# A recommender tower on one core: three PSUM banks for lookups and one for transposes, three lookups ahead of each pair, and the last pair's transposes set between MLP steps

## The reference, cut to what matters

```python
e = jnp.stack([tbl_f[ids[:, f]] for f in range(26)], axis=1)      # [2048, 26, 128]
sd = einsum('bfd,bd->bf', e, dense)                               # 26 dot products with the dense row
ss = einsum('bfd,bgd->bfg', e, e); pairs = ss[:, iu, ju]          # 325 dot products between rows
h = concat([dense, sd, pairs, dense], axis=1)                     # 607 columns
h = relu(h @ W_top1 + b_top1)                                     # 512
h = relu(h @ W_top2 + b_top2)                                     # 256
y = h @ W_top3                                                    # 1
```

## Time and profile before

| what | value |
|---|---|
| median of 3 runs | 382.65 us (378.37 to 382.66) |
| the profiled execution's own time | 384.98 us |
| its span, first to last instruction | 383.2 us |
| mean granted clock of TensorE | 0.969 |
| busy: PE, PEld | 335.0 us (87%), 283.2 us (74%) |
| busy: POOL, ACT, DVE | 259.3, 201.8, 187.4 us |
| moved by DMA | 40.56 MB, mean 106 GB/s |

### The profile page before, as it was taken

How to read it: one execution, slowest core, us unless ns; L and a number is a source line. 1 busy time by engine, 2 the same in 40 slices (tenths; PEclk the granted TensorE clock), 3 DMA queues, 4 the chain that set the end, 5 groups by cost and what they waited for, 6 DMA issues and landing times.

```text
span 383.2 us, 8100 instructions
## 1 busy us (share of the span) xinstructions
PE 335.0 (87%) x3328; PEld 283.2 (74%) x3328; DVE 187.4 (49%) x444; ACT 201.8 (53%) x260; POOL 259.3 (68%) x262
## 2 busy tenths in 40 slices
PE   0798997859899989979989797979989798988976
PEld 0676777748777768868878586968888687978865
DVE  0798973700487744033587572230578473314011
ACT  3387866714563756635461665735472655655201
POOL 5777777777777777777777777777777777730000
PEclk9999998999999999989999899999999899998989
DMA  7997355442255134622136215542226412340310
GB/s 155 254 255 191 118 191 152 116 132 53 54 122 157 49 76 131 159 83 58 50 92 171 74 48 148 117 129 56 50 60 148 126 49 65 90 122 2 90 38 1
DMA packets 46547, 40.56 MB, mean 106 GB/s; under 512 B 29815, under 2 KB 40559, under 8 KB 46512
## 3 DMA queue, kind: packets, MB, share of 16 engines
q1 hardware_dynamic: 38320, 23.26, 23.4%
q0 software_dynamic: 8192, 16.79, 17.1%
HBM read 34.28 MB, written 5.76 MB: 104 GB/s over the span
## 4 chain that ended last, share of the span: by engine, by line
PE 58%; DMA 16%; SPq 9%; POOL 5%; issue 5%; ACT 4%; DVE 2%; ACTq 0%; DVEq 0%
PE oh_ps L504 23%; PE dot_ps L522 15%; PE mlp_ps L543 11%; DMA dots_scratch<-dots 6%; POOL rows L327 5%; SPq L253 5%; PE mlp_ps L552 5%; PE tr_ps L488 4%; SPq L262 3%; DMA ids_bc<-ids_t_dram 3%; DMA zt<-dots_scratch 3%; ACT feat L352 2%; DMA rows<-tbl_dram,idx_sb 2%; ACT feat L360 1%; DMA dots_scratch<-rows 1%
## 5 line engine op out<-in xcount | busy, mean ns | idle before, releaser
L327 POOL DMA_INDIRECT rows<-tbl_dram,idx_sb x256 | 258.8, 1011 | 79.4 <-issue 75.6
L425 DVE TENSOR_SCALAR onehot<-ids_bc 125x512 fp32r<-125x512 int16 x320 | 125.3, 445 | 32.1 <-PE oh_ps L504 24.0
L504 PE MATMUL oh_ps<-onehot,table_hi 125*128 125x512 f32 x320 | 105.5, 411 | 20.2 <-DVE onehot L425 14.4
L504 PE MATMUL oh_ps<-onehot,table_lo 125*128 125x512 f32 x320 | 101.6, 399 | 0.0
L352 ACT ACTIVATE feat<-tr_ps 128x512 f32<-128x512 f32 x64 | 77.3, 1221 | 31.5 <-PE tr_ps L488 30.8
L504 PEld LDWEIGHTS oh_ps<-onehot,table_hi 125*128 125x128 f32 x320 | 59.3, 195 | 33.7 <-issue 12.9
L360 ACT ACTIVATE feat<-oh_ps 128x512 f32<-128x512 f32 x40 | 48.9, 1222 | 45.9 <-PE oh_ps L504 44.8
L504 PEld LDWEIGHTS oh_ps<-onehot,table_lo 125*128 125x128 f32 x320 | 62.1, 194 | 14.0
L522 PE MATMUL dot_ps<-feat 128*54 128x52 f32 x2048 | 61.0, 220 | 10.4 <-issue 5.0
L522 PEld LDWEIGHTS dot_ps<-feat 128*54 128x54 f32 x2048 | 57.8, 136 | 15.1 <-issue 7.6
L543 PE MATMUL mlp_ps<-zt,w_sb 117*128 117x256 f32 x224 | 54.1, 396 | 8.6 <-DMA zt<-dots_scratch 8.6
(11 more groups left out here) (24 smaller groups left out, 55.6 us busy)
## 6 DMA issues: line engine op xcount, KB each, us to landing
ids_bc<-ids_t_dram SPq DMA_DIRECT2D x40, 128.0 KB
dots_scratch<-dots SPq DMA_DIRECT2D x28, 175.5 KB
rows<-tbl_dram,idx_sb POOLq DMA_INDIRECT x256, 2.7
dots<-tbl_dram SPq DMA_DIRECT2D x5, 480.0 KB
zt<-dots_scratch SPq DMA_DIRECT2D x14, 117.0 KB
w_sb<-tbl_dram SPq DMA_DIRECT2D x3, 480.0 KB
dense_sb<-dense_f_dram SPq DMA_DIRECT2D x8, 128.0 KB
zt<-dense_t_dram SPq DMA_DIRECT2D x7, 128.0 KB
```

The costliest lines, as they stand in the source:

```text
L327: nc.gpsimd.indirect_dma_start(rows[:, g, t, :], None, tables[UNIT[u][k]], bass.IndirectOffsetOnAxis(ap=idx_sb[:, n % 2, g * TILES + t:g * ...
L425: last = nc.vector.tensor_scalar(onehot_part(m, part)[:, c, :], ids_bc[0:TP, m % IDSLOTS, :], float(part * PROWS + c), None, ALU.is_equal)
L504: last = nc.tensor.matmul(oh_ps[:, m % 2, :], table[0:TP, u, row * D:(row + 1) * D], onehot_part(m, part)[:, c, :], start=(table is table_ ...
```

## The change

PSUM is divided anew: `oh_ps` gets three banks and `tr_ps` one. Accordingly a lookup waits for the eviction of the lookup three before it, and `transposes` waits for the eviction of the unit just before it. In the orders, the third lookup `l2` moves from behind the dot products of the previous pair's odd chunk to in front of them, for pairs 1 to 3; its eviction `c2` comes behind `c1`, and DVE makes the parts of three lookups ahead of copying those dot products. In the second half of the last pair, the transposes `b2`, `b3` and `b4` each move one MLP step forward.

```diff
+BANKS = 3
-SECOND = "l0 l1 q4 o0 q5 o1 o2 q6 o3 o4 q7 d0 d1 d2 d3 a0 d4 d5 d6 c0 d7 c1 a1 "
-THEN = "l0 a0 l1 a1 d0 d1 d2 d3 d4 d5 d6 c0 d7 c1 "
-LOOK = ("a2 l2 c2 l3 c3 i6 a3 l4 c4 i7 a4 l5 c5 i8 l6 c6 i9 a5 l7 c7 a6 l8 c8 a7 f l9 c9 "
+SECOND = "l0 l1 l2 q4 o0 q5 o1 o2 q6 o3 o4 q7 d0 d1 d2 d3 a0 d4 d5 d6 c0 d7 c1 c2 a1 "
+THEN = "l0 a0 l1 a1 l2 d0 d1 d2 d3 d4 d5 d6 c0 d7 c1 c2 "
+LOOK = ("a2 l3 c3 i6 a3 l4 c4 i7 a4 l5 c5 i8 l6 c6 i9 a5 l7 c7 a6 l8 c8 a7 f l9 c9 "
         "e0 e1 e2 e3 b0 e4 e5 e6 e7 ")
-REST_LAST = "b1 m0 m1 b2 g m2 m3 b3 m4 b4 b5 b6 b7 "
+REST_LAST = "b1 m0 b2 m1 g m2 b3 m3 b4 m4 b5 b6 b7 "
...
-        tr_ps = ps("tr_ps", [P, 2, 2, CH], fp32)
-        oh_ps = ps("oh_ps", [P, 2, BOTH], fp32)
+        tr_ps = ps("tr_ps", [P, 2, CH], fp32)
+        oh_ps = ps("oh_ps", [P, BANKS, BOTH], fp32)
...
-                    for i in range(PLACES, 2 * PARTS):
+                    for i in range(PLACES, BANKS * PARTS):
                         make_part(NO * j + i // PARTS, i % PARTS)
                     if j == 1:
                         layer3(0)
                     dots_to_sbuf(n - 1)
-                    for i in range(2 * PARTS, NO * PARTS):
+                    for i in range(BANKS * PARTS, NO * PARTS):
...
-                if i >= 2:
-                    pe.wait_ge(transposed_out, i - 1)
+                if i:
+                    pe.wait_ge(transposed_out, i)
...
-                if m >= 2:
-                    pe.wait_ge(looked_up_out, m - 1)
+                if m >= BANKS:
+                    pe.wait_ge(looked_up_out, m + 1 - BANKS)
```

More of the change, by code:

```diff
@@ L351, in transposed_to_feat @@
                 act.wait_ge(transposed, i + 1)
-                nc.scalar.activation(feat_view(n % 2, UNIT[u]), tr_ps[:, i % 2], ACT.Copy
+                nc.scalar.activation(feat_view(n % 2, UNIT[u]), tr_ps[:], ACT.Copy
                                      ).then_inc(transposed_out, 1)
@@ L359, in looked_up_to_feat @@
                 both = feat[:, :, :, ONEHOT[m % NO] + 1]
-                nc.scalar.activation(both, oh_ps[:, m % 2, :].rearrange("p (c b) -> p c b", c=2), ACT.Copy
+                nc.scalar.activation(both, oh_ps[:, m % BANKS, :].rearrange("p (c b) -> p c b", c=2), ACT.Copy
                                      ).then_inc(looked_up_out, 1)
@@ L483, in transposes @@
                     pe.wait_ge(ident_made, 1)
-                if i >= 2:
-                    pe.wait_ge(transposed_out, i - 1)
+                if i:
+                    pe.wait_ge(transposed_out, i)
                 for k in range(2):
                     for t in range(TILES):
-                        last = nc.tensor.transpose(tr_ps[:, i % 2, k, t * P:(t + 1) * P], rows[:, 2 * u + k, t, :],
+                        last = nc.tensor.transpose(tr_ps[:, k, t * P:(t + 1) * P], rows[:, 2 * u + k, t, :],
                                                    ident[:])
@@ L503, in lookup @@
                             row = part * PROWS + c
-                            last = nc.tensor.matmul(oh_ps[:, m % 2, :], table[0:TP, u, row * D:(row + 1) * D],
+                            last = nc.tensor.matmul(oh_ps[:, m % BANKS, :], table[0:TP, u, row * D:(row + 1) * D],
                                                     onehot_part(m, part)[:, c, :],
```

## The result

The changed kernel takes 399.63 us (median of 5 runs, 399.26 to 402.21) against 382.65 before: a ratio of 1.0485 with a 95% interval of 1.044 to 1.0531. The profiled execution took 402.21 us, 17.2 more than the one of before; its span is 399.5 us, 16.3 more.

What follows compares the result with a forecast made beforehand. The prediction took PE's work (335.0 us, 87% of the span) plus its waits as the bound. Its terms, 13.6 - 0.2 + 4.7 + 1.3 + 0.3, gave +19.7 us: 404.7 profiled, 402.4 median, range 395 to 409.

Steps and rivals of the forecast that it cites:

- Term 1: Pairs 2 and 3: a4 waits for a3's eviction behind late ids, and l2 delays c0; +6.8 us a pair, +13.6.
- Term 2: End of pair 0: b2 and b3 wait for evictions, but three lookups cover the wait for z; -0.2 us.
- Term 3: Pair 1: a2 waits for a1's eviction, a4 for a3's, and a lookup behind runs slowed; +4.7 us.
- Term 4: Last rows: evictions of b5, b6 and b7 come in series before the last dot products; +1.3 us.
- pair 0: Possible eviction stalls where the margin is thin because ACT also splits tables; +0.3 us taken.
- B: Rival: one bank for transposes costs nothing, so no change; +0.7 us, 383.4 us; chance 0.07.
- A: Rival, faster: ACT evicts a3 before PE reaches a4, so ids don't hold it; -8.6, 374 us; chance 0.03.
- C: Rival, much slower: longer low-clock stretches and stalls at each unit of pair 0; 408 to 414 us; chance 0.06.

Runs made afterwards that it cites:

- e1: Changed kernel with ACT's ids steps i6, i7 and i8 placed behind the evictions of a3 and a4; 390.56 us, ratio 1.0197 to the kernel before.
- e2: Kernel before with one bank for transposes instead of two, orders and two lookup banks unchanged; 394.46 us, ratio 1.0339.
- e3: Changed kernel with SP loading the ids of lookups 6, 7 and 8 ahead of storing and reloading z; 381.93 us, ratio 0.9998 to the kernel before.
- e7: Changed kernel with the last pair's transposes back in their old order; 405.69 us, ratio 1.0649 to the kernel before.
- e5: e3 with POOL leaving out the last two tables' gathers for chunks 1 to 7 (results differ from the reference); 378.49 us, ratio 0.9902 to the kernel before.
- e8: e4 with POOL leaving out the last two tables' gathers for chunks 1 to 7 (results differ from the reference); 375.05 us, ratio 0.9799 to the kernel before.
- e9: Kernel before with only the last pair's transposes spread as in the change; 504.51 us, where the kernel before took 507.01.
- e12: Same kernel as e10, run again; 500.3 us, where the kernel before took 504.6.
- e4: Kernel before with SP loading the ids of lookups 6 and 7 ahead of storing z; 381.22 us, ratio 0.9968.
- e10: e4 with the last pair's transposes spread as in the change; 504.3 us, where the kernel before took 507.01.
- e11: Same kernel as e9, run again; 502.71 us, where the kernel before took 504.6.

## Why the prediction was right, point by point

The time (402.4 forecast, 399.63 measured) and the sign held, and so did the mechanism: `a4` behind `a3`'s eviction behind `i6`, shown by e1, e2 and e3 from three sides. The sum of +19.7 us was 3.4 too high, by errors that partly cancel, and some of its nearness hangs on where the clock happened to fall. Against the terms of the sum the marks give, in us of span:

| term | predicted | measured | from |
|---|---|---|---|
| 1, pairs 2 and 3 | +13.6 | +11.1 | (3.0 + 3.5) + (1.2 + 3.4) |
| 2, pair 0 to pair 1 | -0.2 | -0.4 | c0 of pair 1 |
| 3, pair 1 | +4.7 | +3.6 | 40.9 - 37.3 |
| 4, the last rows | +1.3 | +2.1 | 26.4 - 24.4 |
| pair 0 | +0.3 | in term 2 | |

The measured terms sum to the 16.3 us of the spans but for rounding.

**Term 1** was right in its two parts, 3.1 for the wait and 3.67 for the lookup in front, except that pair 1's second stretch grew by 1.2 and not 3.67. There the kernel before had run `p0` and `p1` slowed, for 5.41 us, after 2.35 us of waiting for `z`, and the one after took 3.73 after 2.02: 1.7 us that the clock took in one execution and not in the other; nothing shows that the edit caused it. Of the other 0.8 us, 0.3 is the shorter wait for `z` and 0.4 a wait for a copy that only the kernel before has there. The waits at `a4` were 8.15 and 8.75 us where 9.1 was forecast, since the ids landed sooner in pair 2 (`i6` 15.7 us after `c0`, not 16.5).

**Term 2** came out at -0.4, and that is in part luck. `b3` started at 73.14 (73.0 forecast), the wait for `z` was gone and `o0` ran at full speed, all as forecast (the 3.10 and 1.73 us were for one step, not two). But the term charged nothing for a lowered clock behind the waits of `b2` and `b3`, and four of the six executions with these waits had one, for some 2.6 us in e1. The profiled execution of the kernel after had not.

**Term 3** was mis-sized in the clock. I charged 1.6 us for a slowed lookup behind the wait at `a4`. That wait lasted 2.8 us and not 4.8, and the two lookups behind it took 7.27 us together, full speed. The clock had fallen earlier, behind `a2`'s wait of 4.28 us, as two windows of the kernel after show (us, busy times, then the granted clock):

```profile
108.00:120.00 12.00, 9.16 (x34) 7.55 (x35) 5.29 (x14) 5.11 (x5) 9.26 (x10) 0.72 0.58 147
120.00:135.00 15.00, 12.21 (x59) 9.87 (x58) 10.42 (x25) 8.68 (x10) 11.65 (x12) 1.00 0.31 89
```

What it cost there was paid out of the wait for ids that followed, so it cost nothing. Without the 1.6 the term is +3.1, and 3.6 was measured. The Trainium skill, "TensorE: Matmul & The Clock Gate", section "What's actually happening", calls the number of slow matmuls at a kernel's start "run-variable". In the middle of this kernel the traces show the like: 3.73 against 5.41 us after nearly the same idle time (e7), and full against lowered clock behind the same two waits (e1).

**Term 4**: the last dot products start 5.85 us after layer 2's end (362.08 from 356.23), 5.8 forecast. The 0.7 us more are their first group, which starts slowed behind the idling.

**The rivals.** B, one bank costs nothing, is refuted by e2: 3.4% for the bank alone. So what the Trainium skill, "TensorE: Matmul & The Clock Gate", section "HAM oscillation — how this bites in real kernels", reports of another kernel, that double-buffering "gave no further gain", doesn't carry over; the measurement decides. What does carry over stands in the Trainium skill on the same page, section "Architectural detail: the array is 16× 32×32, not 1× 128×128": "ACT/DVE are strict FIFO". The trace agrees: `a3` of pair 2 was transposed by 204.9 and evicted from 215.41, 10.5 us behind a step that it had nothing to do with. A did not happen in the changed kernel: `i6` started 15.7 and 16.3 us after `c0`. e3 made its condition true, and its price of 374 was wrong: e3 gave 382. It lacked POOL, which I dismissed in half a sentence ("runs a chunk ahead"); that holds for its buffers, but its issue rate put the last gather at 337 to 339 us in all these kernels that gather everything, except e7 (341.6, after a wait of 5.2 us for PE). Without that bound e5 still stands at 378.5. Its pair 1 still takes 38.3 us from `c0` to copy, against 31.9 and 32.0 in the others, with the wait at `a2` and the lowered clock behind it; that this is the whole of the 4.5 us is not shown. C, much slower, did not happen either: no unit of pair 0 waits for an eviction but `b2` and `b3`.

## What to carry to other kernels

Before taking a buffer away, look at what stands ahead of its eviction in that engine's order, not at how long the eviction takes: 1.2 us of copying held PE for 9, because a DMA wait of another stream came first. Then ask which transfer is late and whether its queue can issue it earlier; two added lines on SP gave back the 17 us here. And price the engine that hardly ever waits (POOL's 256 gathers at 1.3 us) before promising what a cured stall will bring.

## What the runs showed of the hardware beyond that

The kernel before took 382 us in the runs beside e1 to e8 and 505 to 507 us in those beside e9 to e12. The record names chip 4 both for e1 to e4 and for e9 and e10, so the number of the chip does not separate the two conditions, and whether the chip is the cause isn't shown. In the slower one PE stops for 57 us among the dot products of e11 without a releaser that the profile shows, and the mean granted clock is 0.877 in e9 and e11 against 0.969 before. What is missing there isn't settled.
